# Starting every large SBUF tile at a multiple of 512 bytes in a one-core transformer kernel

## What is computed

```
x = x + tanh(g_xattn[0]) * conv_attention(ctx, ctx, norm(x))      # products of k and v, a long convolution, times q
x = x + tanh(g_ffn[0])   * ffn0(norm(x))    # shared 1024-wide SwiGLU + 8 experts of 128, top 2
x = x + tanh(g_xattn[1]) * causal_attention(norm(x), ctx, ctx)    # 16 heads of 16
x = x + tanh(g_ffn[1])   * ffn1(norm(x))    # relu^2; shared 256-wide + 32 experts of 128, top 6
```

## Time and profile before

| | |
|---|---|
| time, median of 3 runs | 899.1 us (896.85 to 900.62) |
| the profiled execution's own time | 895.12 us |
| its span, first to last instruction | 893.3 us |
| TensorE (PE) busy | 871.4 us, 98% of the span |
| weight loads (PEld) busy | 713.0 us, beside the matmuls |
| VectorE (DVE) busy | 591.8 us, 66% |
| ScalarE (ACT) busy | 531.5 us, 60% |
| GpSimd (POOL) busy | 131.2 us, 15% |
| granted TensorE clock | 0.997 of full speed |
| the 16 DMA engines | 106.44 MB, 119 GB/s on average |

### The profile page before, as it was taken

One profiled execution on the slowest core, in us unless ns is written; L12 is line 12 of the kernel. 1 busy time (PEld: TensorE's weight loads), 2 busy tenths in 40 slices (PEclk: granted clock), 3 DMA queues, 4 the chain that ended last, 5 costly groups with the idle time before them and its releaser, 6 DMA issues.

```text
span 893.3 us, 13927 instructions
## 1 busy us (share of the span) xinstructions
PE 871.4 (98%) x4780; PEld 713.0 (80%) x4780; DVE 591.8 (66%) x1228; ACT 531.5 (60%) x914; POOL 131.2 (15%) x110
## 2 busy tenths in 40 slices
PE   7999999999999999889999989999999999999997
PEld 7999887787788888767777777877788888888886
DVE  4998754565745665599999765758655466655664
ACT  2334443444643453557786867767777877777774
POOL 6996100010112110012120400000000000000000
PEclk9999999999999999999999999999999999999999
DMA  8230233336323532023333053444444344444433
GB/s 282 104 119 31 93 90 99 122 107 189 102 100 113 156 115 67 7 62 117 120 116 122 31 167 118 134 141 134 143 137 136 105 126 147 149 151 146 144 118 106
DMA packets 68389, 106.44 MB, mean 119 GB/s; under 512 B 9120, under 2 KB 31936, under 8 KB 67936
## 3 DMA queue, kind: packets, MB, share of 16 engines
q1 hardware_dynamic: 68112, 105.47, 37.4%
q10 hardware_dynamic: 208, 0.09, 0.0%
HBM read 96.79 MB, written 8.74 MB: 118 GB/s over the span
## 4 chain that ended last, share of the span: by engine, by line
PE 88%; DVE 5%; POOL 2%; DMA 1%; issue 1%; ACT 1%; SPq 0%; DVEq 0%; POOLq 0%; ACTq 0%
PE bank L685 39%; PE bank L721 30%; PE bank L1556 3%; PE bank L1567 2%; PE bank L1194 2%; PE bank L1193 2%; PE bank L1459 1%; PE bank L1547 1%; PE bank L369 1%; PE bank L1541 1%; PE bank L1191 1%; PE bank L1212 1%; PE bank L1576 1%; PE bank L350 1%; POOL weighted L1067 1%
## 5 line engine op out<-in xcount | busy, mean ns | idle before, releaser
L482 ACT ACTIVATE y_hi<-y 128x512 fp32r<-128x512 f32 x200 | 124.0, 621 | 81.5 <-DVE y L565 80.8
L579 DVE TENSOR_TENSOR y<-y,gate_rows 128x512 f32<-128x512 f32 x124 | 85.7, 692 | 120.8 <-ACT y L471 118.5
L721 PE MATMUL bank<-y_hi,w_hi 128*128 128x512 f32 x400 | 157.3, 393 | 1.6 <-DVE y_lo L315 1.2
L721 PE MATMUL bank<-y_lo,w_hi 128*128 128x512 f32 x400 | 156.5, 391 | 0.0
L721 PE MATMUL bank<-y_hi,w_lo 128*128 128x512 f32 x400 | 156.0, 390 | 0.0
L315 DVE TENSOR_TENSOR y_lo<-y,y_hi 128x512 fp32r<-128x512 f32 x196 | 134.3, 686 | 29.9 <-ACT y_hi L482 29.6
L465 ACT ACTIVATE activated<-bank 128x512 f32<-128x512 f32 x136 | 81.2, 597 | 81.3 <-PE bank L685 76.6
L685 PE MATMUL bank<-x_hi_first,w_hi 128*128 128x512 f32 x264 | 106.2, 402 | 0.7 <-DVE w_lo L310 0.7
L685 PE MATMUL bank<-x_hi_first,w_lo 128*128 128x512 f32 x264 | 104.2, 395 | 0.0
L685 PE MATMUL bank<-x_lo_first,w_hi 128*128 128x512 f32 x264 | 104.1, 394 | 0.0
L685 PE MATMUL bank<-x_hi_last,w_hi 128*128 128x512 f32 x264 | 104.0, 394 | 0.0
(11 more groups left out here) (156 smaller groups left out, 1358.3 us busy)
## 6 DMA issues: line engine op xcount, KB each, us to landing
gate_rows<-gates SPq DMA_DIRECT2D x156, 256.0 KB, 3.7
w_raw<-in_wu SPq DMA_DIRECT2D x68, 256.0 KB, 2.6
w_raw<-in_wu SPq DMA_DIRECT2D x32, 384.0 KB, 4.4
k_blocks<-k_parts SPq DMA_DIRECT2D x128, 64.0 KB, 2.3
k_parts<-xn_split SPq DMA_DIRECT2D x32, 128.0 KB
v_slot<-in_v_rows SPq DMA_DIRECT2D x16, 256.0 KB, 2.6
ctx_windows<-in_ctx_win SPq DMA_DIRECT2D x3, 1024.0 KB, 13.3
x_mixed<-in_x SPq DMA_DIRECT2D x4, 512.0 KB, 9.2
```

The costliest lines, as they stand in the source:

```text
L482: act.activation(mem.yhi[:, K % S, :], mem.y[:, K % S, :], ACT.Copy).then_inc(s_yh, 1)
L579: dve.tensor_tensor(mem.y[:, K % S, :], mem.y[:, K % S, :], gate, ALU.mult).then_inc(s_yd, 1)
L721: last = pe.matmul(acc(s)[:, c, :], w_[:, Nu % S, wc], y_[:, K % S, :], start=(n == 0 and m == 0), stop=(n == U - 1 and m == 2), skip_grou ...
```

## The change

`sb` keeps count of where the next tile will begin. Ahead of a tile of 512 bytes or more in a partition it makes a gap tile, if one is needed, so that the tile begins at a multiple of 512 bytes. Smaller tiles are placed as before, right behind the one ahead. When the convolution stage's tiles are released the count is set back.

```diff
+SBUF_BASE, LINE = 16512, 512
...
+        place = [SBUF_BASE]
+
         def sb(name, shape, dt=F32, ctx=top):
+
+            bytes_ = math.prod(shape[1:]) * (2 if dt == BF16 else 4)
+            gap = -place[0] % LINE if bytes_ >= LINE else 0
+            if gap:
+                ctx.enter_context(nc.sbuf_tensor(f"gap_{name}", [P, gap // 4], F32))
+            place[0] += gap + (bytes_ + 31) // 32 * 32
             return ctx.enter_context(nc.sbuf_tensor(name, shape, dt))
...
         def context_stage():
             A = Stage()
             pa = ExitStack()
+            below = place[0]
...
             pa.close()
+            place[0] = below
             return A
```

More of the change, by code:

```diff
@@ L12 @@
+import math
 from contextlib import ExitStack
```

## The result

The changed kernel takes 891.04 us (median of 8 runs, 889.36 to 897.35) against 896.93 us for the kernel before in the same comparison (median of 8, 894.20 to 900.62). The ratio is 0.9942, 95% interval 0.9921 to 0.9962: 5.2 us faster, between 3.4 and 7.1. I had forecast 25.8. The time lies in the range, but the gain is off by a factor of five, and the term that made most of it (18.5 us) did not come at all. Rival A's mechanism is the nearest one. That its time (891.8) agrees with 891.04 to within 1 us is luck in part: it was reckoned from the 899.1 us of three runs, where the median of eight is 896.93, and its gain of 7.3 us lies above the interval.

The account below looks back on a forecast made before the run. TensorE's feed-forward matmuls were taken to bound the kernel. 10.9 us from f0 and 15.0 from f1, 25.8 in sum with the first pass's 7.3 included, off 899.1 gave 873.3 us; range 862 to 900.

Parts of the forecast that it names:

- Rival A: Large matmuls: remainder 480 alone slows the first pass, 0 is only as good as 32 or 288; 7.3 us gained, 891.8; chance 0.25.
- What bounds the kernel: TensorE holds 88% of the chain of waits, the two feed-forward products 69%; DMA 1%; the attention is bound by VectorE.
- First pass, down to today's second pass: f0 and f1: first-pass steps fall from 4.18 to 4.08 and 2.78 to 2.72 us, 7.3 us together.
- All large matmuls, below today's 226.7 ns: Both passes of f0 and f1: aligned operands touch one 64-byte piece less, 220.0 ns a matmul; 25.8 us, the 7.3 included.
- The floor of 216: Large matmuls of f0 and f1 at 216 ns each, 37 us less, 862 us; chance 0.08.
- B: First-pass input tiles are slow by their low region or bank of memory, not their remainder; no change, 899.1 us; chance 0.18.
- C: Tiles beginning near a boundary are slow, so 0 is bad: all large matmuls 233.3 ns, 11.3 us more, 910.4; chance 0.11 (any slowdown).
- VectorE, ScalarE, DMA: Other engines and transfers: no effect of the remainder, 0 taken; 2 us either way kept for the attention, DMA at most 1 us.

Follow-up runs that it names:

- the kernels that only slow the matmuls: Against before: y_hi, y_lo and x_last tiles moved to remainder 480, 906.47 us (ratio 1.0116); against the changed kernel: w_hi, w_lo at remainder 32, 907.10 us (1.0114 to before).
- the first experiment: The kernel before with only the first pass's two input tiles moved by 64 bytes, from remainder 480 to 32: 891.47 us, ratio 0.9944.

## Why the prediction was right and wrong

*What bounds the kernel*: right. TensorE's stream is the bound in both layers, and every nanosecond of a large matmul shows: the kernels that only slow the matmuls lie 10.2 and 10.4 us above before, against 11.3 by the count.

*First pass, down to today's second pass*: right in kind, and the whole of the gain. The step values 4.18 to 4.08 and 2.78 to 2.72 came exactly. The sum was mis-sized: 7.3 forecast, 5.4 measured (141.81 to 139.42 us is 2.4 instead of 3.2; 199.15 to 196.10 is 3.0 instead of 4.1; means of three), which agrees with the 5.2 of the runs. I took the gain times all 32 and 68 steps. But of the steps that can be compared some 18 of 31 in f0's first pass gained 0.10 to within 0.01, and some 47 of 67 in f1's gained 0.06. Steps that follow a piece of small work gain less (0 to 0.09 us). Behind the four transposes of line 360 twelve matmuls take 2.75 us in the changed kernel, where they took 2.80, and not 2.72:

```profile
154.72 2.75 PE bank L695 x12
```

From the second to the ninth they come 0.231 us apart and only then 0.227; why is not shown. And a few steps got longer (by up to 0.36 us in f0, 0.14 in f1), because TensorE waits for a y_lo. The clearest is the last but one of f0's first pass. The chain of the changed kernel there:

```profile
221.13 1.28 ACT L506
...
223.22 1.28 ACT L473
...
224.52 0.61 ACT activated L473
...
226.60 0.64 ACT y_hi L492
...
227.26 0.70 DVE y_lo L325
```

Two table loads of ScalarE (for the router's sigmoid and back), 1.28 us each, hold up `activated`, y, y_hi and y_lo. From the first table load to the end of y_lo it is 6.8 us before and after; TensorE, which is faster now, arrives first and waits. The chain starts late as well. In this execution VectorE waited for a gate row one step earlier, and the table load began behind it:

```profile
219.03 0.69 DVE L570 TENSOR_TENSOR y<-activated,gate_rows 128x512 f32<-128x512 f32 x1 [1.47 <-DMA gate_rows<-gates]
...
228.01 0.50 PE L731 MATMUL bank<-y_hi,w_hi 128*128 128x512 f32 x1 [0.38 <-DVE y_lo L325]
```

Against an undisturbed step of its own kernel this step took 0.68, 0.48 and 0.74 us longer in the three executions of the changed kernel, and 0.28 in before. In the second the gate row was in time, so about 0.2 us is what the fixed chain adds; the other 0.2 to 0.26 go with gate rows that held up y by 0.2 to 0.3 us. I had written "I therefore let the whole gain through, and take nothing off" by looking at busy shares; a latency chain is not in them.

*All large matmuls, below today's 226.7 ns*: wrong, and this is the step that failed. It was "the grain explains why 32 costs a piece", so 33 pieces and 220.0 ns. The step of 6.67 ns between the two passes is not a count of 64-byte pieces: aligned operands take 227, start 64 takes 230 and start 128 takes 232 with weights at 0, though all three touch 32 pieces, and both operands at 32 (228.8) are within 1.3 ns of both at 0. The floor of 216 is not seen for fp32r either: it was carried over from plain float32 at half rate, bf16 meets it with 215.8, and no fp32r stream of 512 columns came below 226.7. That made 18.5 us out of nothing: the term measured 0. What spoke against it stood in the rows: 480 is 32 past a multiple of 64, as 32 and 288 are, so it touches 33 pieces too, and it cost one grain more. I gave A 0.25 because I expected straddled boundaries to cost something.

*Why the first pass was slow*: wrong even in rival A, which had a "particular remainder (480)". It is the distance to the weights. For the large matmuls the trace of before had three distances, 0, 256 and 192, and I had looked at the moving operand's column of the table alone. The right reading would have forecast the same 892 us, and also that aligning all tiles is one of many ways to get it.

*B* fell with the first experiment. The 16-byte lines of the Trainium skill ("SBUF — State Buffer", section "Specifications (TRN2)") cannot tell these placements apart; the runs do, by 1.2% on one side and 0.6% on the other. *C* as a mechanism fell as well: a start near a boundary is not what slows. Its price, 11.3 us, is near the 10.2 and 10.4 measured for the placements that are out of step.

*VectorE, ScalarE, DMA*: right on the mean durations and on the first loads, not on all of the path. w_raw's larger loads land in 4.0 to 4.1 us (median) in the changed kernel's three executions, in 4.2 to 4.4 in before's, and in 4.3 in the kernel with the weights 32 off, where w_raw is aligned too; so a gain by alignment is not shown. Gate rows take 3.7 as before, but single late ones and the k_blocks reached the path. The attention moved by about 3 us in the first profile, more than the 2 us that I had set as the limit. Two readings in the prediction are wrong and change nothing: by the earlier trace rows ScalarE is busy 44 to 76% of the four windows (not 61 to 76) and VectorE 56 to 66%, and the 316 ns are not those of line 1191, whose mean in the earlier trace rows is 323 ns, which gives 151 ns in place of 152.

## What to carry to other kernels

Where fp32r matmuls of 512 columns with 128 weight columns bound a kernel, place the moving operands and the weights at the same start modulo 256 bytes; one gap of 64 bytes at the right tile did as much here as aligning everything. Other shapes need their own measurement. Two passes of the same loop that differ in one tile are an experiment that the trace has already made; before extrapolating from it, write down every quantity that differs, distances between operands among them. And when the bound engine gets faster, look for fixed chains (table loads, hand-overs between engines) at each place where it restarts, not only at the shares of the others.

## What the runs showed of the hardware

- fp32r matmuls of 512 columns with 128 weight columns, at a granted clock of 1.00, come every 227 to 230 ns if moving operand and weights start at a distance of 0 modulo 256 bytes, every 232 to 234 ns at the other multiples of 32 tried, but for the moving operand 64 or 320 bytes on, 229.6. Weights 140 KB further up change nothing (228.3 and 233.8 ns).
- fp32r costs 13 to 17 ns above N/2.4 from 256 to 512 columns; bf16 2.5 ns, at every start tried.
- Between 8 and 128 weight columns the rule changes: 230.8 to 231.7 ns at all three distances with 32, and the least at distance 192 with 96 (228.3, against 230.0 at 0).
- In mixed streams the disturbance reaches matmuls whose own distance is 0: 12 at 192 and 6 at 0 cost 232.4 ns on average instead of the 231.1 that 12 x 233.3 and 6 x 226.7 give.
- Waits of weight loads for the same 64 KB loads in the attention vary between 0.7 and 3.3 us in three executions of one program.
